# Graph network block on one Trainium2 core: another order of work in the sorting stage

## The reference, cut to what matters

```python
def _gcn(x, src, dst, W, b, n):
    deg = segment_sum(ones_like(src), dst, n)
    dinv = where(deg > 0, deg ** (-0.5), 0.0)
    norm = dinv[src] * dinv[dst]
    h = x @ W
    return segment_sum(h[src] * norm[:, None], dst, n) + b
...
h = maximum(_layernorm(x), 0.0)          # x: (1024, 512), 16384 edges
src, dst = concat(src, arange(n)), concat(dst, arange(n))
mu, var = mean(h, 0), var(h, 0)
h = (h - mu) * rsqrt(var + EPS) * bn_w + bn_b
h = _gcn(h, src, dst, gcn_in_w, gcn_in_b, n)
for i in range(4):
    h = h + _attn(_ln(h), cond, Wq[i], Wk[i], Wv[i], Wo[i])
    u = _ln(h) @ geglu_w[i] + geglu_b[i]
    val, gate = split(u, 2)
    h = h + (val * gelu(gate)) @ ffo_w[i] + ffo_b[i]
h = _gcn(h, src, dst, gcn_out_w, gcn_out_b, n)
out = x + (h + maximum(_layernorm(x), 0.0))
```

## Time and profile before

| | us |
|---|---|
| median of 3 executions | 2542.01 (2541.48 to 2542.66) |
| the profiled execution | 2540.8 |
| its span | 2539.0 |
| TensorE busy in the span | 2475.8 (98%), 12583 matmuls |
| VectorE, ScalarE, GpSimd busy | 1347.3, 1035.2, 594.6 |
| granted TensorE clock, mean | 0.989 |

### The profile page before, as it was taken

The page is one execution under the profiler, slowest core; times in us unless marked ns, Lnnn a source line. Parts: engine busy times, 40 slices in busy tenths (PEclk is TensorE's granted clock), DMA queues, the critical chain, the costliest instruction groups (busy, mean ns, idle before and its releaser), DMA issues.

```text
span 2539.0 us, 35649 instructions
## 1 busy us (share of the span) xinstructions
PE 2475.8 (98%) x12583; PEld 2056.6 (81%) x12583; DVE 1347.3 (53%) x2665; ACT 1035.2 (41%) x2122; POOL 594.6 (23%) x470
## 2 busy tenths in 40 slices
PE   5879999999999999999999999999999999999999
PEld 3548888888888888888888888888888888888887
DVE  8795766732226776632236677622236667622245
ACT  8873444542223344542224434532223443632223
POOL 2000000144440000154440000154430000154431
PEclk8889999999999999999999999999999999999999
DMA  2012000121111000012111100021110000021130
GB/s 75 1 40 98 34 17 33 34 67 67 65 55 35 34 31 19 34 67 67 66 54 35 34 33 26 26 82 60 66 63 34 17 33 34 26 83 66 64 114 34
DMA packets 29751, 122.04 MB, mean 48 GB/s; under 512 B 3120, under 2 KB 3504, under 8 KB 25008
## 3 DMA queue, kind: packets, MB, share of 16 engines
q1 hardware_dynamic: 29616, 120.31, 13.7%
HBM read 116.10 MB, written 4.19 MB: 47 GB/s over the span
## 4 chain that ended last, share of the span: by engine, by line
PE 92%; DVE 5%; ACT 2%; issue 1%; POOL 0%; DVEq 0%; ACTq 0%; POOLq 0%
PE ps L1488 28%; PE ps L1489 28%; PE ps L1490 28%; PE ps L1675 2%; PE ps L1692 2%; PE ps L1694 2%; DVE oh_d L1135 1%; PE ps L1689 1%; ACT full L763 1%; PE ps L1702 1%; PE ps L1716 1%; ACT d_high L602 0%; DVE oh_s L1133 0%; PE ps L1539 0%; DVE xT_lo L1386 0%
## 5 line engine op out<-in xcount | busy, mean ns | idle before, releaser
L1488 PE MATMUL ps<-xT_hi,wg_hi 128*128 128x512 f32 (+1 forms) x1104 | 414.2, 375 | 1.9 <-DVE xT_lo L1386 1.9
L1489 PE MATMUL ps<-xT_lo,wg_hi 128*128 128x512 f32 (+1 forms) x1104 | 412.5, 374 | 0.0
L1490 PE MATMUL ps<-xT_hi,wg_lo 128*128 128x512 f32 (+1 forms) x1104 | 412.4, 374 | 0.0
L1430 DVE SCALAR_TENSOR_TENSOR ff<-ps,cols_sb,gel 128x512 f32<-128x512 f32 x128 | 96.0, 750 | 574.0 <-ACT gel L859 574.0
L859 ACT ACTIVATE gel<-ps,cols_sb 128x512 f32<-128x512 f32 x128 | 88.1, 688 | 629.9 <-PE ps L1490 629.9
L1439 DVE TENSOR_TENSOR h<-h,ps 128x512 f32<-128x512 f32 x256 | 174.9, 686 | 136.1 <-PE ps L1490 136.1
L1488 PEld LDWEIGHTS ps<-xT_hi,wg_hi 128*128 128x128 f32 x1104 | 207.7, 188 | 39.7 <-DVE xT_lo L1386 2.7
L1490 PEld LDWEIGHTS ps<-xT_hi,wg_lo 128*128 128x128 f32 x1104 | 207.7, 188 | 36.7
L1489 PEld LDWEIGHTS ps<-xT_lo,wg_hi 128*128 128x128 f32 x1104 | 207.8, 188 | 36.5
L437 POOL TENSOR_SCALAR veps<-mv 128x1 f32<-128x1 f32 x65 | 14.2, 218 | 940.4 <-DVE mv L933 940.4
L1488 PE MATMUL ps<-cond_hi,w_hi 128*128 128x512 f32 x512 | 203.7, 398 | 0.0
(11 more groups left out here) (249 smaller groups left out, 5292.4 us busy)
## 6 DMA issues: line engine op xcount, KB each, us to landing
stage<-in_pieces SPq DMA_DIRECT2D x138, 512.0 KB, 3.3
stage<-in_condT SPq DMA_DIRECT2D x33, 1024.0 KB, 4.8
x<-in_x SPq DMA_DIRECT2D x2, 1024.0 KB, 6.5
at_s<-at SPq DMA_DIRECT2D x1, 2048.0 KB, 11.1
at16b<-at_s SPq DMA_DIRECT2D x1, 2048.0 KB, 10.5
out<-h SPq DMA_DIRECT2D x8, 256.0 KB, 2.0
bias_row<-in_rows SPq DMA_DIRECT2D x6, 256.0 KB, 3.7
raw<-in_condT SPq DMA_DIRECT2D x1, 1024.0 KB, 4.7
```

Source lines behind the costliest of these rows:

```text
L1430: dve.scalar_tensor_tensor(ff[:, s % 2, :], ps[:, step_bank(j, a, s, 0), :], cols_sb[:, bass.ds(COL["geglu_b"] + 32 * l + 4 * j + 2 * a + ...
L1488: pe.matmul(bank, l_hi, r_hi, start=(first and i == 0), stop=False)
L1489: pe.matmul(bank, l_hi, r_lo, start=False, stop=False)
L1490: end = pe.matmul(bank, l_lo, r_hi, start=False, stop=(last and i == n - 1))
```

## The change

The sorting stage computes the same; the side work is put at other columns, and some of it on another engine or into other memory.

- **Digit rows.** `d_high` is stored as [32 values, 128 columns] and not [128 columns, 32 values]. ScalarE's 20 planes are written side by side; GpSimd's part is written with a step of 128 elements; TensorE reads the 32 values of an edge column with a step of 128.
- **The chain of x first.** On ScalarE all four `z1_of` stand behind column 3, `x0T_of` behind columns 7 to 14, `w_high` behind 10 and 16. On VectorE all four `z1_by_vector` stand behind column 8, `batch_stats` behind 14, `batch_scale` behind 18. On TensorE `x_transpose` stands behind 4 to 7 and 9 to 12.
- **Four buffers.** The image's pieces have a place each, in `x1`, whose contents are used up by then (`y_place`). VectorE writes pieces 0 and 1, ScalarE 2 and 3, and ScalarE computes all four high parts straight from `x0T` with scale and bias: six passes of 1024 elements behind its sign of column 18. `full` isn't used there any more.
- **Degree.** The 128 matmuls stand in four blocks of 32, behind columns 18 to 21; `deg` is taken at column 26 of VectorE's program.
- **First weight products spread.** `g_product(t)` stands behind columns 23, 35, ..., 107, `xs_of_g(t)` behind 31, 43, ..., 115, `xs_low(t)` behind 36, 48, ..., 120; the last `xs_low` leaves the first flush.
- `strips`, `ge`, `bank_i` move to columns 40, 40 and 64.

```diff
+    G_FIRST, G_STEP = 23, 12
...
-            [("d_low", [P, CHUNKS, 32], f16), ("d_high", [P, CHUNKS, 32], f16)],
+            [("d_low", [P, CHUNKS, 32], f16), ("d_high", [P, 32, CHUNKS], f16)],
...
+        def y_place(k):
+            return x1[:, 2 * k:2 * k + 2, :].rearrange("p a n -> p (a n)")
...
-            d_apart(1, d_high, HIGH_BY_POOL)
+            d_apart(1, d_high[:, 0:HIGH_BY_POOL, :].rearrange("p v c -> p c v"), HIGH_BY_POOL)
...
-                last = act.activation(d_high[:, :, v], d5[:, 1, :], ACT.Copy, bias=-float(v))
+                last = act.activation(d_high[:, v, :], d5[:, 1, :], ACT.Copy, bias=-float(v))
...
             def y_high(k):
-                act.wait_ge(bnf_ok, k + 1)
-                act.activation(yT_hi[:, k, :], full[:, :, :].rearrange("p a n -> p (a n)"), ACT.Copy)\
-                    .then_inc(y_hi, 1)
+                act.wait_ge(bn_ok, 3)
+                act.activation(yT_hi[:, k, :], x0T[:, k, :], ACT.Identity, scale=bn[:, k:k + 1],
+                               bias=bn[:, KC + k:KC + k + 1]).then_inc(y_hi, 1)
+
+            def y_by_scalar(k):
+                act.activation(y_place(k), x0T[:, k, :], ACT.Identity, scale=bn[:, k:k + 1],
+                               bias=bn[:, KC + k:KC + k + 1]).then_inc(y_far, 1)
...
             for c in range(CHUNKS):
                 sign(c)
...
+                if c == 3:
+                    for t in range(4):
+                        z1_of(t)
+                if 7 <= c < 15:
+                    x0T_of(c - 7)
+                if c in (10, 16):
+                    w_high(c // 16, c // 16, attn_place(0, 0, c // 16))
+                if c == 18:
+                    for k in range(KC):
+                        if k >= 2:
+                            y_by_scalar(k)
+                        y_high(k)
+                if c in range(G_FIRST + 8, G_FIRST + 8 + G_STEP * NT, G_STEP):
+                    t = (c - G_FIRST - 8) // G_STEP
...
             def y_of(k):
...
+                dve.wait_ge(bn_ok, 3)
+                dve.tensor_scalar(y_place(k), x0T[:, k, :], bn[:, k:k + 1], bn[:, KC + k:KC + k + 1], ALU.mult, ALU.add)\
+                    .then_inc(bnf_ok, 1)
...
                 if c == 1:
                     x_stats_of(1)
...
+                if c == 8:
+                    for t in range(4, NT):
+                        z1_by_vector(t)
+                if c == 11:
+                    d_equal(d_low[:, :, :], 1)
+                if c == 13:
+                    first_w_low(0)
+                if c == 14:
                     batch_stats()
...
+                if c == 16:
+                    d_equal(d_high[:, :, :], 2)
+                if c == 18:
                     batch_scale()
                     y_of(0)
+                    y_of(1)
+                    y_low(0)
+                if c == 19:
+                    first_w_low(1)
+                if 20 <= c < 23:
+                    y_low(c - 19)
+                if c == 26:
                     dve.wait_ge(deg_mm, 1)
...
+                if c in range(G_FIRST + 13, G_FIRST + 13 + G_STEP * NT, G_STEP):
+                    xs_low((c - G_FIRST - 13) // G_STEP)
...
             for j in range(FLUSH * FLUSHES):
                 one_hots(j)
-                if j == 1:
-                    xs_low(NT - 1)
...
-                if 8 <= c < 12:
-                    x_transpose(c - 8)
+                if 4 <= c < 8:
+                    x_transpose(c - 4)
+                if 9 <= c < 13:
+                    x_transpose(c - 5)
                 if 18 <= c < 22:
-                    x_transpose(c - 14)
...
+                    if c == 18:
+                        pe.wait_ge(d_oh_ok, 2)
+                    for e in range(32 * (c - 18), 32 * (c - 17)):
+                        last = pe.matmul(ps[0:32, 2, 0:32], d_low[:, e, :], d_high[:, :, e], start=(e == 0),
+                                         stop=(e == CHUNKS - 1))
...
-                if c in range(66, 66 + 7 * NT, 7):
-                    t = (c - 66) // 7
+                if c in range(G_FIRST, G_FIRST + G_STEP * NT, G_STEP):
+                    t = (c - G_FIRST) // G_STEP
```

More of the change, by code:

```diff
@@ L447, in d_apart @@
             def d_apart(which, out, n):
-                pool.tensor_tensor(out[:, :, 0:n], d5[:, which, :].unsqueeze(2).broadcast_to([P, CHUNKS, n]),
+                pool.tensor_tensor(out, d5[:, which, :].unsqueeze(2).broadcast_to([P, CHUNKS, n]),
                                    iota0[:, 0:n].unsqueeze(1).broadcast_to([P, CHUNKS, n]),
@@ L1057, in y_of, with y_low @@
             def y_of(k):
[L1058 to L1066 removed]
+                dve.wait_ge(bn_ok, 3)
+                dve.tensor_scalar(y_place(k), x0T[:, k, :], bn[:, k:k + 1], bn[:, KC + k:KC + k + 1], ALU.mult, ALU.add)\
+                    .then_inc(bnf_ok, 1)
+            def y_low(k):
+                if k < 2:
+                    dve.wait_ge(bnf_ok, k + 1)
+                else:
+                    dve.wait_ge(y_far, k - 1)
                 dve.wait_ge(y_hi, k + 1)
[L1068 to L1069 removed]
+                dve.tensor_tensor(yT_lo[:, k, :], y_place(k), bits(yT_hi[:, k, :]), ALU.subtract).then_inc(y_lo, 1)
             dve.wait_ge(pay_ok, 3)
@@ L1108, in _ @@
                     last.then_inc(deg_ok, 1)
+                if c == 40:
+                    strips()
+                    dve.tensor_scalar(ge[0:NT, :], iota0[0:NT, 0:SLOTS], first_c[0:NT, 0:1], None, ALU.is_ge)\
+                        .then_inc(ge_ok, 1)
+                if c == 64:
+                    dve.wait_ge(ge_mm, 1)
+                    dve.tensor_scalar(bank_i[0:1, :], ps[0:1, 3, 0:SLOTS], float(HALF), -float(HALF),
+                                      ALU.mult, ALU.add).then_inc(bank_ok, 1)
+                if c in range(G_FIRST + 13, G_FIRST + 13 + G_STEP * NT, G_STEP):
+                    xs_low((c - G_FIRST - 13) // G_STEP)
             to, of, w, upper = (srt[:, n, :] for n in range(4))
@@ L1541, in _ @@
                 last.then_inc(oh_used, 1)
-                if 8 <= c < 12:
-                    x_transpose(c - 8)
+                if 4 <= c < 8:
+                    x_transpose(c - 4)
+                if 9 <= c < 13:
+                    x_transpose(c - 5)
                 if 18 <= c < 22:
-                    x_transpose(c - 14)
-                if c == 32:
+                    if c == 18:
[3 more added lines that the diff above has]
+                                         stop=(e == CHUNKS - 1))
+                    if c == 21:
+                        last.then_inc(deg_mm, 1)
+                if c == 48:
                     pe.wait_ge(ge_ok, 1)
@@ L1549, in _ @@
                         .then_inc(ge_mm, 1)
[L1550 to L1554, removed]
-                                         stop=(e == CHUNKS - 1))
-                    if c == 57:
-                        last.then_inc(deg_mm, 1)
-                if c in range(66, 66 + 7 * NT, 7):
-                    t = (c - 66) // 7
+                if c in range(G_FIRST, G_FIRST + G_STEP * NT, G_STEP):
+                    t = (c - G_FIRST) // G_STEP
                     if t == 0:
```

43 lines of the change are left out of this document (3 added, 40 removed).

## The result

| | before | after |
|---|---|---|
| median, us (5 executions each) | 2541.48 (2540.68 to 2542.66) | 2553.05 (2552.41 to 2553.63) |
| ratio to before, 95% interval | | 1.0045 (1.003 to 1.006) |
| span of the profiled execution | 2539.0 | 2551.8 |
| granted TensorE clock, mean | 0.989 | 0.989 |

The changed kernel is 11.6 us slower, more than twice the 5.3 us forecast. L numbers in this part are lines of the kernel that the row is from; in the changed kernel the sign is L643, the scatter L1040, a column's matmuls L1549, a digit's L1560, a product L1498 to L1500.

The account below looks back on a forecast made before the run. It took TensorE to bound the last stretch, but gaps and a chain of waits the middle one. Loop +5.4 (10 us gained, given back by spread products), flush -0.6, GpSimd +0.5: +5.3 us, 2547.3 us, range 2541.5 to 2553.

Parts of the forecast that it names:

- GpSimd's stepped write: In preparation, GpSimd's 1536 digit elements written with a step of 128 take 4.4 us instead of 2.77; x_nm at 18.9.
- three signs: Forecast wrong if products follow in 4.9 us or less, clock is full before product 0, or digit matmuls exceed 0.08 us.
- the line: Between weight products, product, eviction and four signs stand in line: 5.55 us for each product; last column at 100.4.
- Planes, first sign: At the start, ScalarE's twenty planes written as rows save 5.3 us; first sign waits for chunk numbers, 15.65, gaining 4.5.
- bn: Scale and shift of x's batch norm, ahead of the image: ready at 37.4 against 44.9, gain 7.5 us.
- Image: After column 18, six ScalarE passes of 1024 elements at 1.12 us, 6.7 us in all, replace the buffer handing.
- Digit matmuls: Four blocks of 32 at columns 18 to 21, 0.056 us a matmul; three blocks on the path, 6.4 us.
- second rival: TensorE's stepped read slows the digit matmuls to twice 0.056 us, +5.4 us: 2552.7, chance 0.12.
- First product: Product 0, behind the digit blocks, starts at 51.5 instead of 61.3 to 61.5: 10 us gained.
- Clock: Product 0 runs at half clock; a rival had the clock fall to 0.50 between products, about 2566, chance 0.03.
- first rival: Digit blocks bring TensorE to full clock before product 0: -3.1 us, +2.2 in all, 2544.2, chance 0.18.
- Low part in the flush: The eighth tile's low part leaves the first one-hots, which VectorE alone paces: -0.6 us.

Follow-up runs that it names:

- first experiment: The changed kernel with GpSimd's part of the high digit written side by side, value outside and column inside: 2548.31 us, ratio 1.0028 to the kernel before.
- last experiment: The changed kernel with VectorE's second half of x's statistics ahead of its first scatter: 2553.18 us, ratio 1.0047 to the kernel before.
- fourth experiment: The changed kernel with the old layout of the high digit for all who write and read it: 2547.55 us, ratio 1.0024 to the kernel before.
- fastest kernel here: The kernel before with side-by-side digit rows, four image places, x's chain fed between columns and products 9 columns apart: 2532.25 us, ratio 0.9963.

## Why the prediction was wrong in size and right in sign

The median went to 2553.05, beyond the upper end of the range by 0.05 us, less than its executions differ among themselves (2552.41 to 2553.63). What failed is the price and the reach of GpSimd's stepped write; none of the three signs that I had named for being wrong (products 4.9 us apart, full clock ahead of product 0, digit matmuls over 0.08) appeared. The sign isn't luck: with the write's cost taken away (first experiment) the kernel is still slower, at 2548.3, 1.0 over my forecast, and what makes it so is the line, as forecast. Step by step:

- **Planes, first sign.** Right: 15.72 against 15.65. The planes gained more than I gave them (20 x 0.20, not 20 x 0.31), but ScalarE spent that waiting 2.85 us for the chunk numbers. The first sign came 4.0 us earlier, not 4.5, since before it had started at 19.69 and not at 20.17.
- **GpSimd's stepped write.** This step failed. I took 4.4 us between 2.77 and 6.0, with a stepped element priced at ScalarE's rate; it took 7.06, beyond my upper end, 2.8 ns an element more and not 2.1. x_nm came at 21.5, not 18.9. The first experiment shows what the write costs in all: 4.9 us of bn, 4.7 of the time. I had left 0.5 in the sum for this write. The transposes that I named as its cover did not cover it: z waits for it on both engines and the statistics for the last eviction.
- **VectorE's scatters under that write.** Overlooked. They took 3.65 us instead of 0.60. The Trainium skill has the rule, SBUF — State Buffer, section Who interferes with whom: GpSimd and VectorE share a port pair, some of VectorE's instructions, tensor_scalar among them, can need it, and whoever issues first holds it for the whole instruction while the other blocks. The trace agrees for the scatters, which are tensor_scalar from SBUF to SBUF (3.65 us against 0.60). The statistics, which the rule's list doesn't name, took their usual 2.47 us under the same write. The power agrees with the rule as well: beside the comparison it took 2.10, which is 1.04 and most of a comparison of 1.14, and 1.04 without it. The last experiment puts the statistics ahead of the scatters, so that none is held for long, and gains nothing; so the held scatters cost nothing that the medians show.
- **bn.** 42.34 instead of 37.4: 4.9 late by the write, about 1.1 by the power that I had set beside the comparison at no price; other handoffs were a little shorter than summed.
- **Image.** Right: passes of 1.13 us from start to start against 1.12; 6.8 us in all against 6.7.
- **Digit matmuls.** 0.060 us each against 0.056, 6.8 us on the path against 6.4: the total came out right by luck. The 0.056 was 0.027 and a quarter of what a group pays once, whatever its size. By the right base it would have been 3.9 us, and the second rival's mechanism, the doubled read, is true: 0.060 against 0.030 by the fourth experiment. Its place was right and its price, 5.4 us, was double the 2.8 measured, as its base was. Advanced Engine Details and Errata, section Memory Cachelines, of the Trainium skill, which I weighed lightly, is borne out by the row.
- **The second rival's number.** Its 2552.7 lies 0.35 us from the median, by chance: it put 5.4 us on top of my sum for the digit matmuls, and they took 0.4 more than in my sum. The time that my sum lacked came mostly from the write.
- **First product.** 56.95 against 51.5: the 10 us gained were 4.3. This is 5.4 of the 6.8 us that I was off at the reading of the sums (107.17 against 100.4).
- **Line between the products.** Right: 5.75 against 5.55. From the start of the product to the eviction it took 3.05, not 2.94; eviction and high part 1.25, four signs and a column 1.45, not 1.35. Seven periods make the other 1.4 us.
- **Clock.** The first product took 4.4 us, not 4.9; the first rival (full clock ahead of it) was wrong, and the clock didn't fall between the products either. The windows of the changed kernel, columns as in its stages:

```profile
57.00:60.00 3.00, 3.00 (x9) 2.41 (x8) 1.68 (x7) 0.71 (x2) 1.64 (x1) 0.50 0.00 0
60.00:61.30 1.30, 1.30 (x6) 0.86 (x4) 0.00 (x0) 0.00 (x0) 0.00 (x0) 0.89 0.00 0
61.30:103.00 41.70, 36.15 (x270) 25.93 (x269) 28.39 (x101) 35.60 (x100) 0.00 (x0) 1.00 0.00 1
```

- **Low part in the flush.** The 0.6 us can't be found. From the sums to the aggregation it is 75.7 us, and 74.3 to 75.6 in the seven runs made from the changed kernel, whose programs are the same there. With the low part in the flush it is 74.6 before, and 75.3 to 76.0 in the three runs made from the kernel before.

What turned an earlier first product into a later end is a count that I worked out for the period but never wrote down for the stretch. ScalarE needs 0.30 us a column, so columns that aren't done when the first product comes have to be paid behind it: before, 67 of 128 were done, after 24. My sum held it through its periods, so it explains the slowdown and not the miss. Two things stay open: why the way from the sums to the aggregation differs by up to 1.4 us between kernels whose programs are the same there, and what sets the moment of the clock's rise.

## What to carry to other kernels

When side work is moved ahead of a paced loop, don't stop at how early the chain ends: count the loop steps done by then and add up the pacing engine's busy and idle time to the end. A layout has three sides, each writer and the reader; a step that frees one engine is paid by the others, here 4.3 us on GpSimd and 2.8 on TensorE for 7.3 on ScalarE, of which its first sign could use 4.0. With GpSimd's side written without a step, the same layout gained 3.3 us on the old order. The fastest kernel here fed the chain between loop steps, with its products spaced by what the slowest engine needs.

## What the runs showed of the hardware

- A stepped write costs GpSimd x2.55 (1536 halves, step of 128 elements: 7.06 against 2.77 us) and ScalarE x2.8 (step of 32: 0.568 against 0.204 us a plane of 128).
- TensorE reading 32 moving columns of halves with a step of 128 elements takes 0.060 us a matmul at half clock, 0.030 without a step, in blocks of 32. In groups of four and of 32 alike about 0.10 us is paid once a group, on top of 0.056 or 0.027 a matmul; that this is the change from one kind of matmul to the other is my reading.
- GpSimd's stepped write stopped VectorE's scatters from SBUF to SBUF (3.65 us against 0.60) but not its statistics (2.47 in both). A GpSimd power of 1.04 us took 2.10 beside VectorE's comparison of 4096 halves (1.14).
